# Head 2's product, head 3's transposes and head 3's product each moved to the middle of a key tile, once, in the first group of heads

## The reference

```python
x = x + tanh(g_xattn[0]) * L0_xattn(layernorm(x), ctx, mask, ...)   # 32 heads of 128
x = x + tanh(g_ffn[0])   * L0_ffn(layernorm(x), ...)                # 4-bit weights, 512x512
x = x + tanh(g_xattn[1]) * L1_xattn(layernorm(x), ctx, ...)         # one head of 512
x = x + tanh(g_ffn[1])   * L1_ffn(layernorm(x), ...)                # 8 adapters and a router
```

```python
h_q = x @ w_q.T;  h_k = ctx @ w_k.T;  h_v = ctx @ w_v.T      # per head 128 columns
score = softmax(where(m, h_q @ h_k.T + position_bias, -inf))
attn = score @ h_v;  out = attn @ w_out.T                    # summed over the heads
return x + out
```

## Time and profile before

| | us |
|---|---|
| median of 3 runs (lowest, highest) | 943.73 (943.26, 944.18) |
| the profiled execution, its own time | 943.65 |
| its span in the trace | 941.9 |
| PE busy | 934.0 (99%), 4818 matmuls |
| DVE, POOL, ACT busy | 595.1 (63%), 497.0 (53%), 403.9 (43%) |
| DMA | 202.60 MB, mean 215 GB/s |

### The profile page before, as it was taken

How to read it: one execution, slowest core, us unless ns; L and a number is a source line. 1 busy time by engine, 2 the same in 40 slices (tenths; PEclk the granted TensorE clock), 3 DMA queues, 4 the chain that set the end, 5 groups by cost and what they waited for, 6 DMA issues and landing times.

```text
span 941.9 us, 15363 instructions
## 1 busy us (share of the span) xinstructions
PE 934.0 (99%) x4818; PEld 791.2 (84%) x4818; DVE 595.1 (63%) x1021; ACT 403.9 (43%) x1088; POOL 497.0 (53%) x463
## 2 busy tenths in 40 slices
PE   8999999999999999999999999999999999999998
PEld 7888788888888888888888888888888888888885
DVE  4788945385538554854476547664576967766654
ACT  5765524352434333423333334433442336658730
POOL 3847574555346453646374636563556326688640
PEclk9999999999999999999999999999999999999999
DMA  8136587775677576767678666867686656223002
GB/s 288 46 126 233 194 290 268 265 264 203 259 259 269 218 267 246 275 248 267 223 268 278 245 245 233 291 244 255 236 278 255 242 205 208 121 97 105 1 1 90
DMA packets 71268, 202.60 MB, mean 215 GB/s; under 512 B 10176, under 2 KB 25024, under 8 KB 70208
## 3 DMA queue, kind: packets, MB, share of 16 engines
q1 hardware_dynamic: 70224, 200.83, 59.4%
q10 hardware_dynamic: 1008, 1.32, 0.4%
HBM read 175.90 MB, written 26.21 MB: 215 GB/s over the span
## 4 chain that ended last, share of the span: by engine, by line
PE 93%; DVE 2%; DMA 2%; ACT 1%; POOL 1%; SPq 0%; issue 0%; DVEq 0%; ACTq 0%
PE bank L1982 27%; PE bank L1998 18%; PE bank L2059 17%; PE bank L2164 11%; PE bank L2031 6%; PE bank L2015 6%; PE bank L1958 3%; PE bank L2188 1%; PE bank L2245 1%; PE bank L2043 1%; PE bank L2309 1%; PE bank L2266 1%; DMA craw<-in_ctx 1%; DVE work_raw L1508 1%; POOL wvo L644 0%; DMA stage<-in_w 0%
## 5 line engine op out<-in xcount | busy, mean ns | idle before, releaser
L2059 PE MATMUL bank<-wvo,ao 128*128 128x512 f32 x768 | 179.7, 391 | 0.0
L1998 PE MATMUL bank<-wvo,ct 128*128 128x512 f32 x768 | 177.7, 390 | 0.0
L1998 PEld LDWEIGHTS bank<-wvo,ct 128*128 128x128 f32 x768 | 143.5, 188 | 29.3
L2059 PEld LDWEIGHTS bank<-wvo,ao 128*128 128x128 f32 x768 | 143.0, 188 | 29.3 <-issue 0.2
L644 POOL TENSOR_TENSOR wvo<-stage,wvo 128x512 fp32r<-128x512 f32 x64 | 85.5, 1358 | 143.2 <-ACT wvo L947 143.2
L1982 PE MATMUL bank<-ring,wkq 128*128 128x512 f32 x648 | 158.2, 391 | 0.0
L1982 PEld LDWEIGHTS bank<-ring,wkq 128*128 128x128 f32 x648 | 120.8, 188 | 24.9
L1469 DVE SCALAR_TENSOR_TENSOR acc<-bank,gated_rows,acc 128x512 f32<-128x512 f32 x128 | 93.1, 742 | 39.1 <-PE bank L2059 38.1
L993 ACT ACTIVATE bank<-bank,nmax 128x128 f32<-128x128 f32 x256 | 88.2, 351 | 62.6 <-DVE nmax L1431 62.6
L1460 DVE TENSOR_TENSOR ao<-bank,ao 128x512 fp32r<-128x512 f32 x64 | 44.0, 691 | 99.1 <-ACT ao L999 99.1
L1491 DVE TENSOR_TENSOR qt<-bank,qt 128x512 f32<-128x512 f32 x98 | 66.4, 690 | 57.0 <-PE bank L1982 55.5
(11 more groups left out here) (189 smaller groups left out, 1507.6 us busy)
## 6 DMA issues: line engine op xcount, KB each, us to landing
ring<-combined SPq DMA_DIRECT2D x214, 512.0 KB, 6.4
stage<-in_w SPq DMA_DIRECT2D x63, 512.0 KB, 4.4
passing<-turned_blocks SPq DMA_DIRECT2D x24, 512.0 KB, 2.9
keyed<-passing SPq DMA_DIRECT2D x96, 128.0 KB, 3.0
combined<-work SPq DMA_DIRECT2D x14, 512.0 KB, 3.6
xraw<-in_x SPq DMA_DIRECT2D x2, 1024.0 KB, 11.5
bias<-in_bias SPq DMA_DIRECT2D x8, 256.0 KB, 5.0
cs<-in_ctx SPq DMA_DIRECT2D x1, 2048.0 KB, 7.5
```

The lines of the kernel that those rows point to most:

```text
L1998: mm = pe.matmul(bank[un_of[m][u] % RING][:, :], ct[:, i, c, b * P:(b + 1) * P], wvo[:, j, c, :], start=(c == 0 and i + j == 0), stop=(c = ...
L2059: mm = pe.matmul(bank[to][:, :], ao[:, h, p, b * P:(b + 1) * P], wvo[:, j, 2 * pair + h, :], start=(h == 0 and p + j == 0), stop=(h == 1 a ...
```

## The change

Three calls that stood between key tiles are handed to `plain` as `midway`, so that each runs after the first six of the tile's twelve matmuls:

```diff
                 plain("k4a")
-                attend(0, 2)
-                plain("k4b")
-                transposes(0)
-                plain("k5a")
-                attend(0, 3)
-                plain("k5b")
+                plain("k4b", lambda: attend(0, 2))
+                plain("k5a", lambda: transposes(0))
+                plain("k5b", lambda: attend(0, 3))
                 for i in range(B, 2 * B):
                     project(0, "first", i)
```

## The result

The changed kernel takes 942.47 us (median of 22 runs, 941.79 to 944.01) where the kernel before takes 943.66 (22 runs, 943.07 to 945.83): 1.19 us less. The ratio is 0.9987 with a 95% interval of 0.9981 to 0.9993, so the gain is clear of the noise and small, between 0.7 and 1.8 us, or 0.13% (within the 0.2% that I had called hard to tell from no change). The forecast was 942.6 us.

The account below looks back on a forecast made before the run. PE, busy 934.0 of 941.9 us, was taken to bound the kernel. Step 1's -1.36 us plus step 5's 0.3 us loss gave -1.1, 942.55 from the profiled 943.65, so a forecast of 942.6 us; range 942.0 to 944.2.

Parts of the forecast that it names:

- The bound: PE is busy 934.0 of 941.9 us, so a change pays only by taking idle time from PE.
- step 1: Six k4b matmuls fill the 1.73 us hole before head 2's product, which waits for `keyed`: worth 1.36 us, 0.37 left.
- Steps 2 and 4: Transposes and head 3's product keep their times; POOL's factors for P1 gain 0.49 us: worth 0, margins 1.2 to 2.2.
- Step 3: Projections 8 to 15 start 1.36 us sooner, needing head 3's first low part: worth 0, margin 0.7 us.
- Step 5: Late N4 piece for P4: SP, held at L528, cannot issue the fetch before 134.3, losing some 0.3 us.
- B: Rival: the N4 fetch queues behind the weight load, landing 3.55 us after it; 943.3 us, chance 0.20.
- A: Rival: full gain, the N4 piece in time through a 3.4 to 3.8 us fetch or SP passing L528 sooner; 942.4, chance 0.15.
- C: Rival: `keyed` usually lands earlier than profiled, so the hole is smaller; about 943.3 us, chance 0.08.
- D: Rival: the N4 fetch takes 5.7 us, a loss of 1.9 us; 944.2 us, chance 0.07.
- E: Rival: the N4 fetch meets a DMA backlog, up to 10.3 us, and PE waits 6.5 us; 948.8 us, chance 0.03.
- F: Rival: no effect, something unseen stops k4b's first half before head 2's product; 943.7 us, chance 0.02.
- signs of being wrong: A new PE wait before projection 8, the product much after 108.5, or rows behind 140 us over 1.4 early or late.

Follow-up runs that it names:

- e2: Changed kernel with head 2's product back between k4a and k4b, only the transposes and head 3's product inside tiles: 943.42 us against 943.58 for the kernel before.
- e5: The changed kernel itself, run again on one chip beside other experiments: 942.16 us against 943.57 for the kernel before.
- e1: Changed kernel with only head 2's product inside a tile, transposes and head 3's product between tiles again: 942.21 us against 943.58 for the kernel before.
- e4: Changed kernel with all three moved steps after nine of their tile's twelve matmuls, not six: 941.93 us against 943.58 for the kernel before.
- e6: Changed kernel, but SP enters its loop only after group 1's third product, so one N4 fetch goes out later: 943.75 us against 943.57 for the kernel before.
- e7: Changed kernel with the four small loads of the router's tables issued earlier, near 116 us: 942.70 us against 943.57 for the kernel before.
- e8: Changed kernel with head 2's product behind seven matmuls of k4b, the other two steps still at six: 941.96 us against 943.57 for the kernel before.
- e3: Changed kernel with all three moved steps after three of their tile's twelve matmuls, not six: 943.31 us against 943.58 for the kernel before.

## Why the prediction was right

**The bound and step 1** held, the size too. Head 2's product did not move, 18 matmuls stand ahead of it, and the matmuls put into the hole are worth their own 0.227 us each: three 0.73, six 1.34 to 1.46, seven 1.60 us by the stretch; e2 shows that nothing else is. The rest of the hole after six is 4.47 - 4.08 = 0.39 us in the change and 0.31 in e5, by the start of the product less 18 matmuls, where I had 0.37. (The rows say 0.23 and 0.15, because they count the modelled end of the last matmul as busy, as with the 1.56 in step 1.)

**Steps 2 and 4** held: the transposes and head 3's product keep their times, and POOL gains its 0.49 us of waiting. e1 shows the transposes without a wait at half the distance.

**Step 3** held, with 0.7 us of margin at six matmuls; e4 spent it.

**Step 5** is where the prediction went wrong, though by little. The mechanism exists: e6 shows that PE waits for this fetch, and e7 shows SP arriving late and 0.3 us lost. But it did not happen in either trace of the change. The step said that SP could not issue the fetch before 134.3, and that 0.3 us would be lost. In the profiled execution SP was past L528 at 132.9, 1.1 us sooner than in the trace I had, because the DMAs it waits for landed sooner; the fetch went out on PE's release at 133.71, took 4.3 us, and landed near 138.0, just in time, by PE's weight loads:

```profile
137.82 0.87 PEld L1982 LDWEIGHTS bank<-ring,wkq 128*128 128x128 f32 x4
```

There is no idle time ahead of any of these four; the second, at 138.07, is the one that waits for the piece. The other traces with an untouched queue and six or more matmuls ahead agree: in e1, e4 and e8 the fetch goes out on PE's release too (SP is past L528 at 132.1 to 132.9). In e5 SP passes at 133.4, so the fetch is late at 134.05, but it takes 3.8 us and nothing is lost. The 134.0 of the kernel before was the latest of all, because one of its two DMAs took 11.7 us; in the other traces it took 10.2 to 11.0. From L528's end SP also needs 0.6 us to the fetch, not the 0.3 I allowed; with that and 134.0 my own sum would have lost 0.6 us. So the term is a matter of the single execution, and 0 in the five just named. The forecast was -1.1 us; the two sets of runs of the changed kernel give -1.19 and -1.41, its two traces -1.34 and -1.46 for the stretch. I had taken one execution's arrival for a constant, which made the sum 0.1 to 0.3 us too cautious. That 942.6 still came within 0.13 us of the median is in part luck: the medians scatter by more than the term.

**The rivals.** B, the fetch held back by the load ahead of it, gave a fixed 3.55 us from the load's landing to its own. Measured it is 2.3 us in the change (135.7 to 138.0) and 3.2 in e7 (135.1 to 138.3), while from its own issue the fetch takes 3.6 to 4.3 us in all of them. B is out as I had put it. The rule I had set beside it, from the Trainium skill, "DMA: Bandwidth & Descriptors", section "Queues, rings and completion order", that each DMA engine takes a queue's descriptors in ring order, isn't refuted by that, but it doesn't give the time: the overlap with the load costs the fetch at most the 0.7 us between 3.6 and 4.3. A, the full gain, at 942.4 as near to the measured 942.47 as the forecast or nearer, is what the change's trace shows up to P4, and for the reason that A gave second: SP passed L528 sooner. I had given it 0.15, less than B. C found nothing for it: `keyed` left a hole of 1.53 us in e2 as well, in another execution, and with six matmuls ahead the rest differs by 0.08 us between traces. In e4 it landed some 0.5 us later, which makes the hole larger, not smaller. D and E did not come; e6 shows that a late landing is paid by PE. F is out by the timeline.

**Two sentences that failed.** I had written that from P4 on PE waits only for what PE itself releases; the wait at 333 us in the change's profile, 0.54 us, is for a DMA. And of my signs of being wrong one came up: the row behind P4 stands 1.45 us earlier than before (138.95, not 140.40), over the 1.4 I had set. 0.11 of it is the offset from the start, and 1.34 is the full gain of A, so it speaks against the loss of step 5 and not against step 1. The fetch at 134.3 to 134.4 and PE's new wait in P4, which I had named as signs of being right, did not show either.

What stays open: the medians of the runs differ from what the stretch says by up to half a us (e3 gains 0.27 where its stretch says 0.73; e6 loses 1.6 where its trace says 1.1), and but for the changed kernel, which has two, I have one trace of each. Waits for N4 in the loop, like the one at 333 us in the change's profile, are a part of that scatter; whether they are all of it wasn't tried.

## What to carry to other kernels

A step that waits for a transfer can be handed to the middle of the tile behind it when that tile writes another bank: what counts is how many matmuls now stand ahead of the wait, and each is worth its own time until the hole is full; more than that buys nothing and brings the consumers of the step nearer to their next deadline. Size the hole as start to start less the work, and look for the same pair of steps at a place without a wait before calling a rest of it a cost of the switch. When PE's row shows no wait, look at the weight load's row too. Before adding a gain up to the end, look for the DMA queue's own waits in the stretch behind it: what arrives there by its own clock doesn't come sooner because PE does.

## What the hardware showed that I had not expected

- The switch from 512-column matmuls to the 128x128 product costs PE nothing that can be seen where nothing is waited for (4.09 us for 18 matmuls of 0.227 in the trace before). The way back costs some 0.11 us: the next six 512-column matmuls take 1.47 us there and not 1.36 (rows below; they follow those at 765.13).
- A short wait for data can be missing from PE's rows and stand in the weight load's alone: 0.47 us in e4 and 0.40 in e8, 0.21 and 0.14 of them lost.
- The second of the two DMAs out of `ring`, in the same queue behind the same DMAs, took 11.7 us in the trace before and 10.2 to 11.0 in the nine others whose queue is the same up to there, a spread as large as the gain that was in question.
- Delaying one 512 KB fetch out of 214 by 1.4 to 2.0 us cost all of the gain: 1.6 us by the medians, 1.1 by the trace (e6).

```profile
770.92 1.63 PE L1982 MATMUL bank<-xb,wkq 128*128 128x512 f32 x6
772.39 1.95 PE L2015 MATMUL bank<-kt,qt 128*128 128x128 f32 x16
```
